# Gathers of the second graph in four parts with a landing wait, and softmax chunks at a shorter stride

## The reference, cut to what matters

```
e = leaky_relu(a_src[src] + a_dst[dst]);  e_max = segment_max(e, dst);  ee = exp(e - e_max[dst])
agg = segment_sum(h[src] * ee / segment_sum(ee, dst)[dst], dst)          # 4 heads x 4 experts
scores = layernorm(agg).mean over heads;  w = softmax(top 2 of 4)
out = sum over experts e of g[e] * (gelu(x @ W1[e] + b1[e]) @ W2[e] + b2[e])
```

## Time and profile before

| | us |
|---|---|
| timed runs | 5196.09, 5227.13, 5219.06 |
| median | 5219.06 |
| profiled execution, span | 6013.1 |
| of it, 715 to 3285 (`gather_mix`) | 2570 |
| of it, 3564 to 5571 (`gat_experts`, gathers and chunks) | 2007 |

### The profile page before, as it was taken

The page is one execution under the profiler, slowest core; times in us unless marked ns, Lnnn a source line. Parts: engine busy times, 40 slices in busy tenths (PEclk is TensorE's granted clock), DMA queues, the critical chain, the costliest instruction groups (busy, mean ns, idle before and its releaser), DMA issues. The chain is left out here.

```text
span 6013.1 us, 46816 instructions
## 1 busy us (share of the span) xinstructions
PE 4326.3 (72%) x14757; PEld 2849.2 (47%) x14757; DVE 2806.5 (47%) x6018; ACT 805.6 (13%) x1519; POOL 2975.4 (49%) x2919
## 2 busy tenths in 40 slices
PE   5999777778779888778886545778687777630077
PEld 3776644444445555555554533445454444420045
DVE  5777466565556545666664621222222222232066
ACT  1111511222200000000000110112121111110022
POOL 0000266666666556677776024555545554466600
PEclk8666888888877788777777556888888888765589
DMA  3110533333344455333336552232223232232078
GB/s 102 48 53 30 145 112 112 113 112 113 107 113 132 141 137 144 91 90 90 90 90 79 177 147 50 81 89 84 69 74 88 83 87 80 60 85 54 11 180 220
DMA packets 257510, 596.30 MB, mean 99 GB/s; under 512 B 86189, under 2 KB 142304, under 8 KB 251903
## 3 DMA queue, kind: packets, MB, share of 16 engines
q0 software_dynamic: 119696, 294.84, 18.8%
q1 hardware_dynamic: 137582, 298.62, 17.9%
HBM read 437.77 MB, written 155.48 MB: 99 GB/s over the span
## 5 line engine op out<-in xcount | busy, mean ns | idle before, releaser
L941 POOL DMA_INDIRECT g_rows<-table,gcn_srcT x1664 | 1770.3, 1064 | 799.3 <-issue 472.8
L1804 POOL DMA_INDIRECT n_rows<-gtab,so_own x1122 | 1092.0, 973 | 885.2 <-DVEq L1923 551.2
L1011 PE MATMUL g_ps<-g_rows,g_hot 128*125 128x256 f32 x3328 | 1103.4, 472 | 225.5 <-issue 169.0
L1296 DVE TENSOR_TENSOR acc<-acc,g_ps 125x256 f32 x1664 | 697.3, 419 | 927.7 <-PE g_ps L1011 508.0
L1011 PEld LDWEIGHTS g_ps<-g_rows,g_hot 128*125 128x125 f32 x3328 | 723.1, 233 | 507.0 <-issue 342.9
L1750 PE MATMUL p_py<-f_w,f_hh 128*125 128x256 f32 x2688 | 678.8, 402 | 265.4 <-issue 261.9
L1744 PE MATMUL p_ph<-f_xfT,f_w 128*128 128x500 f32 x1344 | 627.7, 618 | 256.2 <-ACT f_hh L1975 128.5
L1750 PEld LDWEIGHTS p_py<-f_w,f_hh 128*125 128x125 f32 x2688 | 533.6, 199 | 426.8 <-issue 352.8
L1947 DVE TENSOR_TENSOR p_ob<-p_py,p_xb 125x512 f32<-125x512 f32 x168 | 114.7, 690 | 1299.9 <-remote 793.0
L1744 PEld LDWEIGHTS p_ph<-f_xfT,f_w 128*128 128x128 f32 x1344 | 268.8, 201 | 580.5 <-issue 433.2
L471 PE MATMUL a_pdeg<-so_x 125*100 125x125 bf16 x1600 | 372.5, 407 | 41.2 <-DVE so_x L552 41.2
(11 more groups left out here) (330 smaller groups left out, 4373.4 us busy)
## 6 DMA issues: line engine op xcount, KB each, us to landing
o_d<-p_ob SPq DMA_DIRECT2D x21, 1920.0 KB
z_ob<-o_d SPq DMA_DIRECT2D x21, 1920.0 KB
g_rows<-table,gcn_srcT POOLq DMA_INDIRECT x1664
n_rows<-gtab,so_own POOLq DMA_INDIRECT x1122
gout<-n_o SPq DMA_DIRECT2D x33, 408.0 KB
xnT_d<-a_xnT SPq DMA_DIRECT2D x25, 500.0 KB, 2.9
m_area<-xnT_d SPq DMA_DIRECT2D x25, 500.0 KB
qT_d<-m_area SPq DMA_DIRECT2D x25, 500.0 KB
```

Source lines behind the costliest of these rows:

```text
L941: pool.indirect_dma_start(out=rows[:, g % RING, j], out_offset=None, in_=K.table, in_offset=bass.IndirectOffsetOnAxis(ap=K.gcn_srcT[:, 4 * ...
L1011: mm = pe.matmul(ps[q, p % 4, b], hot[:, g % 4, 2 * j + b], rows[:, g % RING, 2 * j + b], start=True, stop=True, skip_group_check=True)
L1296: dve.tensor_tensor(a, a, ps[q, p % 4, b], ALU.add).then_inc(add_s, 1)
L1804: pool.indirect_dma_start(out=rows[:, c % 3, j], out_offset=None, in_=K.gtab, in_offset=bass.IndirectOffsetOnAxis(ap=K.gat_src[:, c * W + ...
```

## The change

Three edits, all in `gat_experts`.

1. A chunk's 34 gathers are issued in four parts of 9, 9, 8 and 8. Ahead of each part POOL waits until the part before the previous one has landed (across chunks too). The wait for `eaten` stays.
2. Each buffer has four landing semaphores, one for each part, instead of one: 12 instead of 3. DVE waits for four instead of one before `n_am`. Nine more semaphores are cleared at the end.
3. `at_unit[c]` is `4 + 12*c // 5`, one chunk in 2.4 units. All 33 chunks are placed, the last at unit 80; the part after the units is empty.

```diff
-    at_unit = [4 + 31 * c // 10 for c in range(chunks) if 5 + 31 * c // 10 < units]
+    at_unit = [4 + 12 * c // 5 for c in range(chunks) if 5 + 12 * c // 5 < units]
...
-        got = [m.gather_sem(f"n_got{s}") for s in range(3)]
+        got = [[m.gather_sem(f"n_got{s}_{b}") for b in range(len(PARTS))] for s in range(3)]
...
-                    for j in range(W):
-                        pool.indirect_dma_start(out=rows[:, c % 3, j], out_offset=None, in_=K.gtab,
-                                                in_offset=bass.IndirectOffsetOnAxis(
-                                                    ap=K.gat_src[:, c * W + j:c * W + j + 1], axis=0)
-                                                ).then_inc(got[c % 3], 16)
+                    j = 0
+                    for b, size in enumerate(PARTS):
+                        c0, b0 = (c, b - 2) if b >= 2 else (c - 1, b - 2 + len(PARTS))
+                        if c0 >= 0:
+                            pool.wait_ge(got[c0 % 3][b0], 16 * PARTS[b0] * (c0 // 3 + 1))
+                        for _ in range(size):
+                            pool.indirect_dma_start(out=rows[:, c % 3, j], out_offset=None, in_=K.gtab,
+                                                    in_offset=bass.IndirectOffsetOnAxis(
+                                                        ap=K.gat_src[:, c * W + j:c * W + j + 1], axis=0)
+                                                    ).then_inc(got[c % 3][b], 16)
+                            j += 1
...
-                    dve.wait_ge(got[s], 16 * W * (c // 3 + 1))
+                    for b, size in enumerate(PARTS):
+                        dve.wait_ge(got[s][b], 16 * size * (c // 3 + 1))
```

More of the change, by code:

```diff
@@ L1761, in gat_experts @@
     chunks = GC // W
+    PARTS = (9, 9, 8, 8)
+    assert sum(PARTS) == W
     units = EARLY * NE
-    at_unit = [4 + 31 * c // 10 for c in range(chunks) if 5 + 31 * c // 10 < units]
+    at_unit = [4 + 12 * c // 5 for c in range(chunks) if 5 + 12 * c // 5 < units]
     with ExitStack() as ctx:
```

## The result

| | before | after |
|---|---|---|
| timed runs, median | 5219.06 us | 5233.90 us |
| ratio of timed runs, 95% interval | | 1.004 [1.0024, 1.0055] |
| profiled execution, span | 6013.1 us | 5218.9 us |
| profiled execution, mean granted clock | 0.772 | 0.827 |

The change makes the kernel slower by 0.4%, 12 to 29 us. That lies inside the forecast's range and within its 1%, but on the other side: the forecast was 5 us faster.

The account below looks back on a forecast made before the run. POOL's issue of gathers was taken to bound the stage in timed runs. From 5219 us, 29 lost at the stage's end and 34 gained by the stride gave 5214 us, bounds 5164 to 5269, stated range 5060 to 5290.

Parts of the forecast that it names:

- POOL's cadence bounds the stage: Second graph's gathers: POOL issues one per 1.278 us, 43.4 us per chunk, so the stage takes at least 1433 us.
- The freeze: In long gather trains of the trace PE, DVE and ACT stop, units take 20.8 us, not 13.6; mostly absent from timed runs.
- The accounting: Whole span: 6013.1 less 877.6 us of POOL's waits gives 5135.5, leaving 83.6 us up to the timed 5219.06.
- the stride's gain: Second graph's stage: 2.4 instead of 3.1 units per chunk gains 33.7 us, bounds 0 and 83.6, if units exceed 14.0 us.
- the unplaced 83.6 us: Timed median beyond the span without POOL's waits; taken as the only trace of units longer than 14.0 us.
- The end: After the stage's last gather: 42.6 us of remaining work and store instead of 13.6, 29 us lost; 50 at PE clock 0.50.
- Landing waits at no cost: POOL's 130 added waits before parts of gathers: none should bind, and an already satisfied wait costs nothing.
- Rival 3: Landing waits bind at each part's first gather once a landing takes over 10.2 us: +94 us, 5313; chance 0.07.
- Rival 1: Units partly slow in timed runs too; at 16 us per unit the change gains 139 us, 5080; chance 0.25.
- Rival 2: Gathers are cheaper without the profiler, say 1.0 us each; the change gains 170 us, 5049; chance 0.12.
- Rival 4: The change does nothing beyond the stage's longer end: 5248, inside the forecast's range; no chance of its own.
- The signs named for "right": Profile after: POOL's wait for `eaten` near zero, no seven-chunk block without PE, two to three units behind the last gather.

Follow-up runs that it names:

- wait_last: Kernel after, with each part of gathers waiting for the part just issued to land, not the last but one; timed 1.0721 of the kernel before.
- before_again: The kernel before, profiled and timed once more without an edit; timed 0.9993 of the kernel before, profiled span 5201.0 us.
- parts_only: Kernel after with the stride put back to 3.1 units, keeping the four parts and landing waits; timed 0.9998 of the kernel before.
- drop_before: Kernel before with the last 6 of 34 gathers left out in each chunk from 3 on (180 gathers); timed 0.9836 of the kernel before.
- b2_28: Kernel before with a stride of 2.8 units and bias b2 added on PE by a one-row matmul, p_xb gone; timed 1.0182 of the kernel before.

## Why the prediction was wrong, step by step

- **POOL's cadence bounds the stage: right.** Forecast 1433 us of gathers, 1439.1 measured; `wait_last` shows POOL's idle time lost one for one.
- **The freeze belongs to the profiled execution: right**, by `before_again`. The reasons given for it were half right. The accounting worked; but the records of a profile do not bring it by themselves. The Trainium skill's rule (NOTIFIC — the notification-queue block, 7.1 and 7.4) allows a profiled run to be held back, it does not say that every one is, and 13 of 14 profiles here show none of it.
- **The failed step is the stride's gain**, "I give this stage its share by gathers, 1122 of 2786, or 33.7 us gained", out of "the unplaced 83.6 us". The gain supposed units longer than 14.0 us. They take 13.6, and POOL waits 0 us for `eaten` in `before_again`. The 83.6 were elsewhere: `gather_mix` is 249.0 us shorter without the freeze, not the 326.4 of its two waits in the earlier trace rows, since POOL still waits 69.7 for `g_ps` there and its issue gaps are 15.7 longer. That places 77, and 18 are no more than the span of this execution below the median. A remainder was turned into a gain in the stage under study without a row that put it there.
- **The stride did gain, by another mechanism** that no step or rival had: 20.1 us of shorter gathers, as fewer of them begin beside `p_xb` and `n_x`. That some gain stood against the end at all is luck, not the forecast's reasoning. The earlier trace rows had the sign of it: 973 ns in the mean where single gathers are 0.94, and L2025's are 944.
- **The end: right in mechanism, sized a little low.** +29 forecast, 49.1 - 16.3 = +32.8 measured. The work behind the last gather took 32.8 (29.6 forecast): the landing's 1.8 us had been left out; ACT took 2.9 instead of 4.2, as its first table load lay ahead of the wait; and `up` took 9.82 instead of 6.87, since PE came out of 13 us of idle time at a granted clock of 0.50 (4738 to 4743 us) and had 1.00 only from 4748 on, so that the 21.0 us grew by 2.8 and did not double. The large store landed after 12.9 us (13 forecast). What follows up to the next gather, 3.4 us here and 2.8 in `before_again`, was left out on both sides; the 0.6 between them fits the nine more semaphores ("under 1 us").
- **Landing waits at no cost: nearly.** 4.7 us of idle instead of 0, and about 2.6 of longer gathers. Rival 3's mechanism, and its condition of a landing over 10.2 us, is met at four of 130 waits; its price was set ten times too high. A wait that is already satisfied shows no cost: `parts_only`.
- **Rival 1** (slow units) fell with `before_again`; its mechanism, with the units made the longer, is what `drop_before` and `b2_28` show. **Rival 2** (cheaper gathers in a timed execution) fell too: the profiled execution of `before_again` is itself one of the ten timed ones, 5202.72 us against a median of 5213.91, and its gathers take 0.977 + 0.305 us. **Rival 4**, "nothing beyond the end", gave 5248, 14 us off where the forecast was 20 off.
- **The signs named for "right"** (no wait for `eaten`, no block of seven chunks without PE, two to three units behind the last gather) all came, while the time went the other way. They could not tell: the wait for `eaten` is 0 in `before_again` too, and the other two follow from the order of the list.

With the measured terms: -20.1 (gathers) + 4.7 (waits) + 32.8 (end) = +17.4, against 17.5 in the stage, 17.9 in the span and 12 to 29 timed. The forecast's sum was -33.7 + 0 + 29; it missed by 13.6 us at the stride, 4.7 at the waits and 3.8 at the end, all in the same direction.

## What to carry to other kernels

When a profiled span stands well above the timed median (15% here), profile the same kernel once more before reading waits from it. Where an engine's cadence bounds a stage, price a new order of the rest by what then stands behind that engine's last item; pace the other work so that it is done shortly before it (here a stride of 2.5 or 2.6, not 2.4). And give a remainder of an accounting to no stage unless a row puts it there.

## What the runs showed of the hardware

- A gather that begins while DVE runs an operation with both inputs in SBUF ends 0.81 to 0.82 us after `p_xb` (56 of 59 in `before_again`) and mostly 0.77 to 0.78 after `n_x`, and takes up to 1.96 us instead of 0.94. One that began before DVE's operation, or within 0.04 us of the start of `p_xb` (3 there, 15 after), is not touched, nor is one beside `p_ob`, which reads PSUM (75 cases).
- The lag from a gather's end to the reader of its data is 1.7 us undisturbed. Beside a 2000 KB store it was 5.7 to 5.9 us for five chunks after, and 11.1 to 11.3 us at the four landing waits that bind.
- A one-row fp32 matmul of 256 columns takes 0.43 us in the trace, and there are two records of it for each written.
- A profile can hold a disturbance that adds 812 us and that the next profile of the same kernel doesn't have; its cause is open.
